# A post-norm layer with linear attention and eight routed experts: row transfers issued by fours, the norms' roots by a power on GpSimd, and merged VectorE instructions

## The chip, the cores and the metric

The kernel runs on one core of one Trainium2 chip. A core has five engines that run their own instruction streams and meet only at semaphores: TensorE (PE, matrix products; its weight loads are listed as PEld), VectorE (DVE), ScalarE (ACT), GpSimd (POOL) and SyncE (SP, which here only issues transfers). The metric is the device time of one execution in microseconds (us); lower is better.

## The reference, cut to what matters

The input is 4 sequences of 512 tokens with 256 features, all in float32.

```python
Q = relu(x @ Wq.T + bq); K = relu(x @ Wk.T + bk); V = x @ Wv.T + bv     # 16 heads of 16
Q, K = Q * decay, K * decay
KV = einsum('bhnd,bhne->bhde', K, V);  Ksum = K.sum(axis=2)
Z = 1 / (einsum('bhnd,bhd->bhn', Q, Ksum) + EPS)
a = (einsum('bhnd,bhde->bhne', Q, KV) * Z) @ Wo.T + bo
x1 = layernorm(x + a)                                      # (v - mean) / sqrt(var + 1e-5)
probs = softmax(x1 @ w_gate); the two largest of 8 experts, their weights made to sum to 1
routed = sum over the two of weight * (silu(g) * u) @ w_down[e],   g, u = x1 @ w_gate_up[e]
shared = (silu(gs) * us) @ w_sh_down,                              gs, us = x1 @ w_sh_gate_up
out = layernorm(x1 + routed + shared)
```

## The kernel before, in words

Float32 products are made of three products of a high and a low part (`split3`, lines 332 to 334), so nearly every operand is first copied into a high part by ScalarE or GpSimd and then subtracted into a low part by VectorE or GpSimd. The order of work on each engine is written out by hand; no scheduler moves anything, and each engine takes its own list in order.

**Attention.** A loop runs over the four sequences b = 0 to 3. On TensorE sequence b has `k_t_v` (L373), the key and value products of sequence b+1, `attend` (L387) for its four tiles of 128 tokens, `proj_q` of b+1, `o_transposed` (L400), `x1_transposed` of b-1 (L426), `proj_o` and the `router` of b-1 (L437). In sequence 3, which has no successor, the first pieces of the shared expert (`shared_gu`) stand between these. VectorE does `kvm_out` (masks the key-value product, L960 and L961, needed by `attend`), `o_out` for each tile (L969, L970, L974), `ot_lo_out` (L985), and `moments`, which adds the residual (L999) and takes mean and variance (L994, L1005). Then comes `x1_norm`, a chain of 12 VectorE instructions on 4 columns that finds 1/sqrt(var + eps) by an integer guess and three Newton steps (`rstd`, L214 to L227). ScalarE's `x1_apply` (L710) applies it. The call of `x1_norm` for sequences 0 and 1 stands in the middle of the next sequence's `o_out`, for sequence 2 ahead of `kvm_out` of sequence 3, and for sequence 3 behind its `moments`.

**Routing and rows.** `top_two` (L1014 to L1030) picks two experts a token, `ranks` on TensorE (L449, L451) counts them, `slots` (L1069 to L1078) turns that into row numbers. GpSimd's `scatter(b)` then writes every token's row of 1032 bytes to two places in HBM: eight indirect transfers of 128 rows (L1318), one behind the other. In between GpSimd splits the feed-forward weights (`split_chunk`, L1301 and L1303, 18 chunks), and makes low parts (`x1_lo`, L1309). SyncE waits for all scatters before it loads the first tile of expert rows (L298).

**Shared expert.** For each sequence four column blocks: `shared_gu` on TensorE, `shared_sg` (L729) on ScalarE, `shared_h` (L1039) on VectorE, `shared_hh` (L736) on ScalarE, `shared_lo` (L1045) on VectorE, then `shared_dn` on TensorE and `shared_out` (L1057) on VectorE, which adds tile by tile into `x1`. Sequences 0 and 1 come before the routed experts, 2 and 3 after them.

**Experts and end.** 40 tiles of 128 rows run through gate, up and down products; results are scattered back (L1345), added up (L1358, L1222), and the second norm is taken: on GpSimd for sequences 0 to 2 by the same Newton steps in 16 instructions each time, on VectorE for sequence 3 (L214 to L227 again), then applied (L859, L1237) and stored (L321).

Of the kernel before, what the change touches and what calls it, by code (L numbers as in the profile page):

```python
# [10 lines left out]
I32 = mybir.dt.int32  # L11
U32 = mybir.dt.uint32
ALU = mybir.AluOpType
# [3 lines left out]
P = 128  # L17
NB, SEQ, D = 4, 512, 256
KD = D // P
# [44 lines left out]
RSQRT_MAGIC = 0x5F3759DF  # L64


def build(nc, xT, x, watt, batt, bq, wffn, wgate, consts, out):
# [5 lines left out]
    with ctx:  # L73
# [36 lines left out]
        warm = sb("warm", [P, 2])  # L110
        stat = sb("stat", [P, TB, 6])
# [98 lines left out]
        def rstd(v, link, h, fused):  # L210


            va, y, t, m = (nw[:, h, n, :] for n in range(4))
            link(v.tensor_scalar(va, mv[:, h, :, 1], EPS_LN, None, ALU.add))  # L214
            link(v.tensor_scalar(y.bitcast(I32), va.bitcast(I32), -0.5, float(RSQRT_MAGIC), ALU.mult, ALU.add))
            for _ in range(3):
                if fused:
                    link(v.scalar_tensor_tensor(t, y, -0.5, y, ALU.mult, ALU.mult))
                    link(v.tensor_tensor(t, t, va, ALU.mult))  # L219
                    link(v.scalar_tensor_tensor(y, t, 1.5, y, ALU.add, ALU.mult))  # L220
                else:
                    link(v.tensor_tensor(t, y, y, ALU.mult))
                    link(v.tensor_tensor(t, t, va, ALU.mult))
                    link(v.tensor_scalar(t, t, -0.5, 1.5, ALU.mult, ALU.add))
                    link(v.tensor_tensor(y, t, y, ALU.mult))
            if fused:
                return v.scalar_tensor_tensor(m, mv[:, h, :, 0], -1.0, y, ALU.mult, ALU.mult)  # L227
            link(v.tensor_tensor(m, mv[:, h, :, 0], y, ALU.mult))
            return v.tensor_scalar(m, m, -1.0, None, ALU.mult)
# [97 lines left out]
        def _(pe):  # L327
# [292 lines left out]
            pe.wait_ge(S["sres_out"], EARLY_B * TB)  # L620
# [278 lines left out]
        def _(dve):  # L899
# [53 lines left out]
            def kvm_out(b):  # L953
# [4 lines left out]
                for m in range(KD):  # L958
                    o = bank[4][:, m * (P + 1):(m + 1) * (P + 1)]
                    v.tensor_tensor(kvm[:, m, 0:P], o[:, 0:P], blk, ALU.mult)  # L960
                    last = v.tensor_scalar(kvm[:, m, P:P + HB], headm, o[:, P:P + 1], None, ALU.mult)  # L961
                last.then_inc(S["kvm_out"], 1)

            def o_out(b, t):

# [454 lines left out]
```

## Time and profile before

| what | us |
|---|---|
| median of 3 runs | 292.87 (292.04 to 293.07) |
| span of the profiled execution, first to last instruction | 284.3 |
| median less span | 8.6 |
| PE busy | 233.3 (82%) |
| DVE busy | 170.2 (60%) |
| POOL busy | 143.5 (50%) |
| ACT busy | 123.3 (43%) |
| mean granted TensorE clock | 0.930 |

Of the profiled execution only the span is shown; a time of its own around it is not. A row of the timeline has start, duration, engine, line, operation, what it writes and reads, the shape and the count, and in brackets how long the engine had stood idle before it and what ended that. "remote" there means that the releasing update could not be tied to an instruction near it. Ends of matmuls are modelled. TensorE, the busiest engine, still stands idle or runs at half its clock in several places, and the table of waits says who ends each pause.

### The profile page before, as it was taken

The page shows a single profiled execution, that of the slowest core. Times are in us where ns is not written, and L with a number is a line of the kernel's source. Part 1 is how long each engine was busy: PE and PEld are TensorE (multiplying, and loading weights), DVE is VectorE, ACT ScalarE, POOL GpSimd, SP SyncE. Part 2 cuts the span into 40 slices and gives each one's busy share as a digit, 9 for nine tenths or more (in the row PEclk, how much of TensorE's full clock was granted, in tenths as well). Part 3 has the DMA queues.
Part 4 walks back from the last instruction along what each step waited for, and adds up shares of the span by engine and source line. Part 5 has one row for each costly group of instructions (what it writes and reads, how often), then busy time and mean ns, then how long its engine had stood idle before and what let it go on. Part 6 is the DMA issues. An engine that isn't in the chain of part 4 may idle for free.

```text
span 284.3 us, 5136 instructions
## 1 busy us (share of the span) xinstructions
PE 233.3 (82%) x1420; PEld 199.2 (70%) x1420; DVE 170.2 (60%) x603; ACT 123.3 (43%) x315; POOL 143.5 (50%) x176
## 2 busy tenths in 40 slices
PE   8799999699794779298783889999999889995370
PEld 3488798598593659285763878888888778894370
DVE  2915467369738857637936256666655524699635
ACT  2252613903630370432024166666765634832730
POOL 0035583797779047258740015665655560748700
PEclk9889999999988699879997899999999999999685
DMA  6913064223421002112352025455554306650242
GB/s 192 379 55 94 0 204 168 75 74 111 129 98 37 2 0 106 42 59 93 120 178 77 0 74 164 139 165 149 162 149 152 109 11 205 241 149 0 71 152 74
DMA packets 21580, 31.72 MB, mean 112 GB/s; under 512 B 3248, under 2 KB 14257, under 8 KB 21556
## 3 DMA queue, kind: packets, MB, share of 16 engines
q1 hardware_dynamic: 17552, 22.46, 26.0%
q0 software_dynamic: 3456, 8.43, 8.6%
q10 hardware_dynamic: 548, 0.53, 0.6%
q8 instruction: 13, 0.21, 0.3%
q14 instruction: 11, 0.09, 0.1%
HBM read 19.70 MB, written 12.76 MB: 114 GB/s over the span
## 4 chain that ended last, share of the span: by engine, by line
PE 54%; DVE 21%; issue 10%; ACT 6%; another core or an unknown queue 6%; DMA 2%; ACTq 0%; DVEq 0%
PE bank L332 16%; PE bank L334 13%; PE bank L333 12%; PE bank L578 3%; PE bank L373 2%; DVE stat L1230 2%; DVE nw L219 2%; DMA k_sb<-in_batt 2%; PE bank L599 2%; ACT xt_hi L736 2%; DVE xt_raw L1039 2%; PE bank L426 1%; DVE x L1222 1%; PE bank L437 1%
## 5 line engine op out<-in xcount | busy, mean ns | idle before, releaser
L1345 POOL DMA_INDIRECT y_pairs<-x_t,dst x40 | 39.4, 985 | 49.1 <-ACT x_t L814 24.9
L332 PE MATMUL bank<-wf_hi,ot_hi 128*128 x120 | 41.1, 342 | 4.1 <-DVE ot_lo L1183 3.0
L1318 POOL DMA_INDIRECT x_slots<-x,slot x32 | 31.7, 991 | 17.6 <-DVE slot L1078 8.9
L332 PE MATMUL bank<-wf_hi,xt_hi 128*128 128x256 f32 x64 | 20.4, 319 | 16.4 <-DVE xt_lo L1045 10.7
L333 PE MATMUL bank<-wf_lo,ot_hi 128*128 x120 | 33.8, 282 | 0.0
L334 PE MATMUL bank<-wf_hi,ot_lo 128*128 x120 | 33.8, 281 | 0.0
L332 PEld LDWEIGHTS bank<-wf_hi,ot_hi 128*128 128x128 f32 x120 | 22.5, 188 | 10.9 <-issue 9.9
L332 PE MATMUL bank<-x1t_hi,wf_hi 128*128 128x512 f32 x64 | 26.7, 418 | 1.2 <-ACT x_t L719 1.2
L332 PEld LDWEIGHTS bank<-wf_hi,xt_hi 128*128 128x128 f32 x64 | 14.2, 223 | 17.6 <-issue 17.6
L333 PE MATMUL bank<-x1t_lo,wf_hi 128*128 128x512 f32 x64 | 25.9, 405 | 0.0
L736 ACT CAST xt_hi<-xt_raw 128x512 fp32r<-128x512 f32 x16 | 9.7, 618 | 37.3 <-remote 11.9
L334 PE MATMUL bank<-x1t_hi,wf_lo 128*128 128x512 f32 x64 | 25.8, 403 | 0.0
L1303 POOL TENSOR_TENSOR wf_lo<-stage,wf_hi 128x512 fp32r<-128x512 f32 x18 | 23.2, 1287 | 1.4
L333 PEld LDWEIGHTS bank<-wf_lo,ot_hi 128*128 128x128 f32 x120 | 22.8, 190 | 0.0
L334 PEld LDWEIGHTS bank<-wf_hi,ot_lo 128*128 128x128 f32 x120 | 22.6, 188 | 0.0
L685 ACT ACTIVATE k_sb<-bank,cst 128x256 f32<-128x256 f32 x16 | 7.6, 475 | 33.7 <-PE bank L348 33.2
L1181 DVE SCALAR_TENSOR_TENSOR dst<-o_sb,te_f 128x1 f32 (+1 forms) x40 | 8.8, 221 | 19.5 <-issue 13.7
L333 PE MATMUL bank<-wf_lo,xt_hi 128*128 128x256 f32 x64 | 19.9, 311 | 0.0
L334 PE MATMUL bank<-wf_hi,xt_lo 128*128 128x256 f32 x64 | 19.8, 310 | 0.0
L804 ACT ACTIVATE q_t<-bank 128x128 f32<-128x128 f32 x40 | 11.1, 278 | 19.9 <-PE bank L334 19.9
L799 ACT CAST ot_hi<-bank 128x256 fp32r<-128x256 f32 x40 | 15.0, 378 | 9.2 <-PE bank L578 8.8
L1293 POOL TENSOR_TENSOR xt_lo<-xt_raw,xt_hi 128x512 fp32r<-128x512 f32 x6 | 7.5, 1276 | 18.4 <-ACT xt_hi L676 18.4
(179 smaller groups left out, 648.8 us busy)
## 6 DMA issues: line engine op xcount, KB each, us to landing
o_sb<-x_slots SPq DMA_DIRECT2D x40, 129.0 KB
stage<-in_wffn SPq DMA_DIRECT2D x18, 256.0 KB, 2.8
x<-in_x SPq DMA_DIRECT2D x4, 512.0 KB, 7.1
out<-x SPq DMA_DIRECT2D x8, 256.0 KB, 2.3
xt_raw<-in_xT SPq DMA_DIRECT2D x3, 512.0 KB, 6.4
x_slots<-fill SPq DMA_DIRECT2D x9, 129.0 KB, 4.5
x<-in_watt SPq DMA_DIRECT2D x4, 256.0 KB, 5.9
k_sb<-y_pairs SPq DMA_DIRECT2D x2, 512.0 KB, 3.7
```

Of the source, the lines that this page charges most:

```text
L332: mm(o, w_hi, m_hi, start=start, stop=False, **more)
L333: mm(o, w_hi, m_lo, start=False, stop=False, **more)
L334: return mm(o, w_lo, m_hi, start=False, stop=stop, **more)
L578: last = nc.tensor.transpose(o[:, k * P:(k + 1) * P], xg[:, u, k * P:(k + 1) * P], ident)
L685: activation(k_sb[:, t, :], o[:, 0:D], ACT.Relu, scale=cst[:, C_DEC + t:C_DEC + t + 1])
L736: copy(hh_hi[:, c, :], hf[:, i % 2, :]).then_inc(S["shh_out"], 1)
L799: copy(xe_hi[:, u % 2, :, :], bank[(4, 7)[u % 2]][:, 0:KD * P].rearrange("p (k n) -> p k n", k=KD)).then_inc(S["xe_hi_out"], 1)
L804: activation(eg[:, u % 2, :], bank[u % 2][:, 0:IM], ACT.Silu).then_inc(S["eg_out"], 1)
L1181: v.scalar_tensor_tensor(dst[:, bass.ds(j, 1)], xg[:, u, D + 1:DT], te_f[:, bass.ds(j + (RING - 1), 1)], xg[:, u, D:D + 1], ALU.not_equal, ...
L1303: g.tensor_tensor(wf_lo[:, c], stage[:, i % 2, :], wf_hi[:, c].bitcast(F32), ALU.subtract).then_inc(S["wf_split"], 1)
L1318: pool.indirect_dma_start(out=x_scat, out_offset=bass.IndirectOffsetOnAxis(ap=slot[:, j, t:t + 1], axis=0), in_=x1[:, t, :], in_offset=Non ...
L1345: pool.indirect_dma_start(out=y_scat, out_offset=bass.IndirectOffsetOnAxis(ap=dst[:, j:j + 1], axis=0), in_=ey[:, u, :], in_offset=None, b ...
```

## The change

Four edits. (1) The chain in `rstd` becomes four GpSimd instructions, one of them a power with exponent -0.5 from a new constant tile; all norms, those of the attention and the last one included, are now GpSimd's, each at a fixed place in its list. (2) `scatter(b)` is cut into two parts of four transfers. Those of sequence 0 have other work between them. From sequence 1 on, GpSimd waits until a part has landed (`landed`) before it issues the next. (3) `kvm_out` makes two instructions in place of four, `o_out` one product for each tile in place of two. (4) `shared_out` adds two tiles at once, and the semaphore `sres_out` counts pairs.

```diff
+        power = sb("power", [P, NB, TB])
-        def rstd(v, link, h, fused):
-            va, y, t, m = (nw[:, h, n, :] for n in range(4))
-            link(v.tensor_scalar(va, mv[:, h, :, 1], EPS_LN, None, ALU.add))
-            link(v.tensor_scalar(y.bitcast(I32), va.bitcast(I32), -0.5, float(RSQRT_MAGIC), ALU.mult, ALU.add))
-            for _ in range(3):
-                if fused:
-                    link(v.scalar_tensor_tensor(t, y, -0.5, y, ALU.mult, ALU.mult))
-                    link(v.tensor_tensor(t, t, va, ALU.mult))
-                    link(v.scalar_tensor_tensor(y, t, 1.5, y, ALU.add, ALU.mult))
...
+        def rstd(g, link, h):
+            va, y, m = nw[:, h, 0, :], nw[:, h, 1, :], nw[:, h, 3, :]
+            link(g.tensor_scalar(va, mv[:, h, :, 1], EPS_LN, None, ALU.add),
+                 g.tensor_scalar(m, mv[:, h, :, 0], -1.0, None, ALU.mult))
+            link(g.tensor_tensor(y, va, power[:, h, :], ALU.pow))
+            return g.tensor_tensor(m, m, y, ALU.mult)
...
-                        pe.wait_ge(S["sres_out"], TB * (b - 1) + 2 * (t // 2) + 2)
+                        pe.wait_ge(S["sres_out"], 2 * (b - 1) + t // 2 + 1)
...
+                o = bank[4][:, 0:KD * (P + 1)].rearrange("p (m n) -> p m n", m=KD)
+                v.tensor_tensor(kvm[:, :, 0:P], o[:, :, 0:P], blk.unsqueeze(1).broadcast_to([P, KD, P]), ALU.mult)
+                v.tensor_tensor(kvm[:, :, P:P + HB], o[:, :, P:P + 1].broadcast_to([P, KD, HB]),
+                                headm.unsqueeze(1).broadcast_to([P, KD, HB]), ALU.mult).then_inc(S["kvm_out"], 1)
...
+                v.tensor_tensor(o_sb[:, t, 0:D].rearrange("p (k h e) -> p k h e", k=KD, h=HB),
+                                o[:, :, 0:P].rearrange("p k (h e) -> p k h e", h=HB),
+                                zt.unsqueeze(3).broadcast_to([P, KD, HB, DH]), ALU.mult).then_inc(S["o_out"], 1)
...
-            x1_norm(b - 1)
             kvm_out(b)
             top_two(b - 2)
...
+            def landed(b, part):
+                pool.wait_ge(S[f"scattered{b}"], 16 * TOPK * (TB // 2) * (part + 1))
...
                     if b == 2 and n == 4:
-                        scatter(0)
+                        scatter(0, 0)
                         x1_lo(b - 1)
+                        x1_norm(2)
                     split_chunk(done)
                     done += 1
+                    if b == 2 and n == 4:
+                        scatter(0, 1)
...
+                    if n == 5 and b == 0:
+                        x1_norm(0)
                     if n == 3 and b == 1:
                         x1_lo(b - 1)
+                        x1_norm(1)
+            scatter(1, 0)
             x1_lo(NB - 2)
-            scatter(1)
-            scatter(2)
+            x1_norm(3)
+            landed(1, 0)
+            scatter(1, 1)
+            landed(1, 1)
+            scatter(2, 0)
             x1_lo(NB - 1)
-            scatter(3)
+            landed(2, 0)
+            scatter(2, 1)
+            landed(2, 1)
+            scatter(3, 0)
+            landed(3, 0)
+            scatter(3, 1)
...
+            pool.wait_ge(S["bn_out"], 4 * TB)
+            rstd(g, link, slice(3, 4)).then_inc(S["ln_last_out"], 1)
```

How this moves instructions, in two places. First VectorE at the mask of sequence 3 (kvm). Before, from the last Newton step of sequence 2's norm (nw, the last four of its twelve instructions) to the router's copy (logit):

```order
L218 SCALAR_TENSOR_TENSOR nw<-nw 128x4 [waits dve_chain]
L219 TENSOR_TENSOR nw<-nw 128x4 [waits dve_chain]
L220 SCALAR_TENSOR_TENSOR nw<-nw 128x4 [waits dve_chain]
L227 SCALAR_TENSOR_TENSOR nw<-mv,nw 128x4 [waits dve_chain]
L960 TENSOR_TENSOR kvm<-bank,cst 128x128 [waits num_mm,kvp_mm]
L961 TENSOR_SCALAR kvm<-cst,bank 128x8
L960 TENSOR_TENSOR kvm<-bank,cst 128x128
L961 TENSOR_SCALAR kvm<-cst,bank 128x8
L1014 COPY logit<-bank 128x32 [waits lg_mm]
```

And after, from the moments (BN_AGGR) of sequence 2 on:

```order
L988 BN_AGGR mv<-stat 128x2 x3
L946 TENSOR_TENSOR kvm<-bank,cst 128x2x128 [waits num_mm,kvp_mm]
L947 TENSOR_TENSOR kvm<-bank,cst 128x2x8
L993 COPY logit<-bank 128x32 [waits lg_mm]
L997 MAX top_v<-logit 128x8 [waits lg_out]
```

The twelve norm instructions are gone from in front of the mask, and the mask is two instructions long. Second GpSimd from its 17th weight chunk to the experts, where x_slots is the scatters' target, x1t_lo a low part and nw a norm. Before:

```order
L1303 TENSOR_TENSOR wf_lo<-stage,wf_hi 128x512 [waits wf_split]
L1309 TENSOR_TENSOR x1t_lo<-x_t,x1t_hi 128x512 [waits x1hi_out]
L1309 TENSOR_TENSOR x1t_lo<-x_t,x1t_hi 128x512
L1318 DMA x_slots<-x,slot 17536x258 [waits x1_out,tags_out,slots_out]
L1318 DMA x_slots<-x,slot 17536x258 x7
L1318 DMA x_slots<-x,slot 17536x258 [waits x1_out,tags_out,slots_out]
L1318 DMA x_slots<-x,slot 17536x258 x7
```

And after, for the same work and up to the first part of sequence 2:

```order
L1281 TENSOR_TENSOR wf_lo<-stage,wf_hi 128x512 [waits wf_split]
L1300 DMA x_slots<-x,slot 17536x258 [waits x1_out,tags_out,slots_out]
L1300 DMA x_slots<-x,slot 17536x258 x3
L1287 TENSOR_TENSOR x1t_lo<-x_t,x1t_hi 128x512 [waits x1hi_out]
L1287 TENSOR_TENSOR x1t_lo<-x_t,x1t_hi 128x512
L213 TENSOR_SCALAR nw<-mv 128x4 [waits mom_out]
L214 TENSOR_SCALAR nw<-mv 128x4
L215 TENSOR_TENSOR nw<-nw,power 128x4 [waits pool_chain]
L216 TENSOR_TENSOR nw<-nw 128x4 [waits pool_chain]
L1300 DMA x_slots<-x,slot 17536x258 [waits scattered1]
L1300 DMA x_slots<-x,slot 17536x258 x3
L1300 DMA x_slots<-x,slot 17536x258 [waits tags_out,x1_out,slots_out,scattered1]
```

The norm of sequence 3 now stands between the two halves of the scatter of sequence 1, so the second half can't start before sequence 3's moments are there, and each later half waits for the landing of the one before.

## Rows read from the trace of the kernel before

**Rows 1.** Waits of TensorE, whole span: total us, times, longest us.

```profile
PE bank L332 <- DVE xt_lo L1045: 10.7, 2, 7.6
PE bank L332 <- DVE x L1057: 5.7, 1, 5.7
PE bank L387 <- DVE kvm L961: 5.5, 1, 5.5
PE bank L426 <- ACT x L710: 5.1, 1, 5.1
```

**Rows 2.** Timeline of ScalarE: x1_apply of sequences 0, 1 and 2.

```profile
49.46 2.08 ACT L710 ACTIVATE x<-x,nw 128x256 f32<-128x256 f32 x4 [1.28 <-DVE nw L227]
73.81 2.08 ACT L710 ACTIVATE x<-x,nw 128x256 f32<-128x256 f32 x4 [2.51 <-DVE nw L227]
93.36 2.07 ACT L710 ACTIVATE x<-x,nw 128x256 f32<-128x256 f32 x4 [11.97 <-DVE nw L227]
```

**Rows 3.** Timeline of VectorE: norm of sequence 2, then the mask.

```profile
87.39 1.18 DVE L214 TENSOR_SCALAR nw<-mv 128x4 f32<-128x4 f32 x1
...
93.25 0.29 DVE L960 TENSOR_TENSOR kvm<-bank,cst 128x128 f32<-128x128 f32 x1
```

**Rows 4.** Timeline of TensorE around attend of sequence 3.

```profile
88.18 0.40 PE L334 MATMUL bank<-x1t_hi,wf_lo 128*128 128x512 f32 x1
94.07 2.18 PE L387 MATMUL bank<-kvm,q_t 128*128 128x136 f32 x8 [5.50 <-DVE kvm L961]
```

**Rows 5.** Timeline of GpSimd: the x1_lo in the norm's time, scatter 1's fifth and last.

```profile
85.99 2.54 POOL L1309 TENSOR_TENSOR x1t_lo<-x_t,x1t_hi 128x512 fp32r<-128x512 f32 x2
...
110.70 0.96 POOL L1318 DMA_INDIRECT x_slots<-x,slot  x1 [0.30 <-issue]
...
114.51 0.96 POOL L1318 DMA_INDIRECT x_slots<-x,slot  x1 [0.31 <-issue]
```

**Rows 6.** Timeline of TensorE, 109.8 to 142.6: router, shared blocks, first products of shared_dn.

```profile
109.82 1.84 PE L437 MATMUL bank<-wg_sb,x_t 128*128 128x8 f32 x16
...
114.15 0.39 PE L334 MATMUL bank<-x1t_hi,wf_lo 128*128 128x512 f32 x1
...
142.58 0.28 PE L334 MATMUL bank<-wf_hi,xt_lo 128*128 128x256 f32 x1
```

**Rows 7.** Timeline of VectorE: a residual add, the router's copy, the slot cast.

```profile
110.02 0.42 DVE L999 TENSOR_TENSOR x<-bank,x 128x256 f32<-128x256 f32 x1
...
116.92 0.19 DVE L1014 COPY logit<-bank 128x32 f32<-128x32 f32 x1 [2.38 <-remote]
...
132.33 3.12 DVE L1078 CAST slot<-slot_f 128x8 uint32<-128x8 f32 x1
```

**Rows 8.** Timeline of ScalarE: shared blocks that wait for TensorE.

```profile
117.05 0.60 ACT L729 ACTIVATE xt_raw<-bank 128x512 f32<-128x512 f32 x1 [1.85 <-remote]
...
147.41 1.14 ACT L736 CAST xt_hi<-xt_raw 128x512 fp32r<-128x512 f32 x2 [11.94 <-remote]
```

**Rows 9.** Windows: length, busy of PE, PEld, DVE, ACT, POOL, PEclk, DMA share, GB/s.

```profile
116.00:117.00 1.00, 0.00 (x0) 0.00 (x0) 0.08 (x1) 0.00 (x0) 0.00 (x0) 1.00 0.37 132
```

**Rows 10.** The same columns, in stretches of 2 us.

```profile
120.00:122.00 2.00, 2.00 (x14) 1.94 (x13) 0.94 (x4) 0.34 (x1) 0.00 (x0) 0.50 0.00 0
...
134.00:136.00 2.00, 0.00 (x0) 0.00 (x0) 2.00 (x3) 1.08 (x2) 1.68 (x3) 1.00 0.00 0
```

**Rows 11.** Timeline of SyncE: first loads of expert tiles.

```profile
150.29 14.37 SPq L298 DMA_DIRECT2D o_sb<-x_slots  x5
```

**Rows 12.** Timeline of VectorE at the end: the last norm's first and last instruction.

```profile
277.85 0.17 DVE L214 TENSOR_SCALAR nw<-mv 128x4 f32<-128x4 f32 x1
...
280.03 0.16 DVE L227 SCALAR_TENSOR_TENSOR nw<-mv,nw 128x4 f32<-128x4 f32 x1
```

**Rows 13.** Timeline of GpSimd: two norm instructions on 4 columns.

```profile
269.19 0.20 POOL L223 TENSOR_TENSOR nw<-nw 128x4 f32<-128x4 f32 x1
269.47 0.19 POOL L224 TENSOR_SCALAR nw<-nw 128x4 f32<-128x4 f32 x1
```

More of the change, by code:

```diff
@@ L972, in o_out @@
                     dve.wait_ge(S["ot_mm"], b)
-                for m in range(KD):
-                    last = v.tensor_tensor(
-                        o_sb[:, t, m * P:(m + 1) * P].rearrange("p (h e) -> p h e", h=HB),
-                        o[:, m, 0:P].rearrange("p (h e) -> p h e", h=HB),
-                        zt[:, m, :].unsqueeze(2).broadcast_to([P, HB, DH]), ALU.mult)
-                last.then_inc(S["o_out"], 1)
+                v.tensor_tensor(o_sb[:, t, 0:D].rearrange("p (k h e) -> p k h e", k=KD, h=HB),
+                                o[:, :, 0:P].rearrange("p k (h e) -> p k h e", h=HB),
+                                zt.unsqueeze(3).broadcast_to([P, KD, HB, DH]), ALU.mult).then_inc(S["o_out"], 1)
             def ot_lo_out(b):
@@ L1127, in _ @@
                     o_out(b, t)
-                    if b >= 1 and t == 1:
-                        x1_norm(b - 1)
                     if b >= 2 and t == 2:
@@ L1276, in _, with link, x1_norm @@
             g.memset(fill[:, 0:D], 0.0).then_inc(S["pool_chain"], 1)
+            g.memset(power[:, :, :], -0.5).then_inc(S["pool_chain"], 1)
             pool.wait_ge(S["cst_in"], 16)
             g.tensor_copy(fill[:, D:DT], cst[:, C_FILL:C_FILL + TAG]).then_inc(S["pool_chain"], 1)
-            pool.wait_ge(S["pool_chain"], 2)
+            pool.wait_ge(S["pool_chain"], 3)
             pool.sem_inc(S["fill_made"], 1)
-            chain = [2]
-            def link(ins):
-                chain[0] += 1
-                ins.then_inc(S["pool_chain"], 1)
+            chain = [3]
+            def link(*instructions):
+                for ins in instructions:
+                    chain[0] += 1
+                    ins.then_inc(S["pool_chain"], 1)
                 pool.wait_ge(S["pool_chain"], chain[0])
+            def x1_norm(b):
+                pool.wait_ge(S["mom_out"], TB * (b + 1))
+                rstd(g, link, slice(b, b + 1)).then_inc(S["nw_last_out" if b == NB - 1 else "nw_out"], 1)
             def split_x_lo(b):
@@ L1310, in x1_lo, with scatter @@
                                     ALU.subtract).then_inc(S["x1lo_out"], 1)
-            def scatter(b):
-                pool.wait_ge(S["slots_out"], b + 1)
-                pool.wait_ge(S["tags_out"], 2 * (b + 1))
-                pool.wait_ge(S["x1_out"], TB * (b + 1))
-                for t in range(b * TB, (b + 1) * TB):
+            def scatter(b, part):
+                if part == 0:
+                    pool.wait_ge(S["slots_out"], b + 1)
+                    pool.wait_ge(S["tags_out"], 2 * (b + 1))
+                    pool.wait_ge(S["x1_out"], TB * (b + 1))
+                half = TB // 2
+                first = b * TB + part * half
+                for t in range(first, first + half):
                     for j in range(TOPK):
```

45 lines of the change are left out of this document (11 added, 34 removed).

## The prediction

> **What bounds the kernel now.** I read the waits of TensorE first, then the timelines of the engines that end them, in order of time. The profile's page has TensorE busy for 233.3 of the span's 284.3 us, so a gain must come from its pauses and from stretches at the lower clock. Its long pauses are few: 5.5 us for the mask, 5.1 us for the applied norm, 5.7 us for the shared addition, and twice for the shared expert's low part, once 7.6 us in the tail and once the other 3.1 us [rows 1]. Each has a cause behind the engine named.
>
> The mask (5.5 us) stands behind sequence 2's norm on VectorE, which runs from 87.39 to 93.25, 5.9 us for twelve tiny instructions [rows 3]; one such chain undisturbed takes 2.34 us (277.85 to 280.19) [rows 12]. Its first instruction took 1.18 us in place of 0.17 [rows 3, 12], while GpSimd ran 512-column subtractions [rows 5]. The chain is held by GpSimd's work, so its price on VectorE is 2.4 to 5.9 us a time.
>
> The next pauses share a stranger cause: TensorE's completions arrive late. The router's products were recorded from 109.82 to 111.66 and shared_gu's last one to 114.54 [rows 6]. VectorE was free, but copied the logits only at 116.92 [rows 7], and ScalarE's SiLU began at 117.05 [rows 8], 2.5 us after its product. A residual add that waited for TensorE at 110.02 came on time [rows 7]. What changed between is the fifth of eight row transfers, issued at 110.70; the eighth was issued at 114.51 [rows 5], and its 132 KB moved in 116 to 117 [rows 9]. So lateness begins with the fifth transfer in a row and ends when they have all landed. It repeats in the last scatter: shared_dn's last product ended at 142.86 [rows 6], ScalarE's cast that waited for it ran at 147.41 [rows 8].
>
> **The change part by part.** The sum is made in the profiled span of 284.3 us. I take the 8.6 us between it and the median of 292.87 as constant, so what leaves the span leaves the median.
>
> *Norm 0.* In sequence 1 ScalarE stood idle for 1.28 us for the norm [rows 2], and TensorE waited behind ScalarE. On GpSimd the norm stands behind the sixth weight chunk, in an idle stretch, and is ready earlier. Gain 1.3 (0 to 1.3).
>
> *Norm 1.* The same, with 2.51 us of ScalarE's idle time [rows 2]. Also VectorE no longer holds back the slots and the last o_out, for which TensorE waited. It works without pause before and behind, so not all comes back. I take 2.2 (0 to 3).
>
> *Norm 2 and the mask.* TensorE's last product ahead of attend began at 88.18, and attend itself at 94.07 [rows 4], 5.9 us later. The mask's input came from TensorE earlier, so attend starts at about 88.2. It took 2.18 us [rows 4] at the lower clock; without the pause the clock should not have fallen, which halves that. Gain 5.9 + 1.1, and 0.1 for the merged mask: 7.1 (4 to 7.5). What is late next? The norm itself: GpSimd has four transfers (each 1.3 us), x1_lo of 2.54 us [rows 5], then the norm. By this count its result is there at 88.5 in place of 93.3, and ScalarE's x1_apply (2.07 us [rows 2]) ends at 90.6, ahead of the transposition that needs it. The lower end is that GpSimd is 3 us later.
>
> *Groups of four, at 114.5.* If no more than four transfers are in a row, completions are on time. SiLU goes from 117.05 to 114.6: 2.4 us (0 to 2.5). The pause before the transposition shrinks from 5.1 us [rows 1] to 2.7. In the pause of 3.1 us later the granted clock stayed 1.00 (2.4 GHz), behind the one of 5.1 us it was 0.50 (1.2 GHz) [rows 10]. TensorE works all through that stretch [rows 10], by my count for 4.8 us, of which full clock gives back at most half; a part is bound by weight loads. I take 2.1 (0 to 2.4).
>
> *At 133.7.* shared_dn waited 3.1 us for the low part. VectorE had the ranks late, and then its slot cast took 3.12 us [rows 7], held by an x1_lo that followed the scatter directly. In the new order the ranks are on time, and x1_lo falls ahead of TensorE's need. Gain 3.0 (0 to 3.1).
>
> *At 142.9 to 154.1.* ScalarE's cast moves from 147.41 to 142.9. Counted on through the next two blocks (product, SiLU, product with the gate, cast, low part) the shared addition is 2.2 us earlier, 0 if lateness stays. The pause of 5.7 us [rows 1] becomes 3.5. Whether the clock then stays up lies between the two pauses above; the slow products there cost about as much as those above, I take 0.9 (0 to 2.2).
>
> *The last norm.* VectorE: 2.34 us [rows 12]. GpSimd: an instruction on 4 columns takes 0.20 us and the next begins 0.28 us after it [rows 13], so four take 1.1 us. The power is not in the trace. Its lower bound is 0.20 like the others, its upper bound a whole 512-column instruction, 1.3 us [rows 5]. It has only 4 columns, so I take 0.4, near the small rows: 1.3 us and a gain of 1.0 (0 to 1.2). The norms of sequences 0 to 2 in the tail are hidden behind shared blocks.
>
> *Merged products.* o_out lies beside TensorE's products nearly everywhere; if that cover goes it is 0.07 us a tile. Three shared_out calls stand on the path. With both, 0.1 (0 to 0.3).
>
> *The new waits.* The fourth transfer lands 2.5 us after its issue, as the eighth at 114.51 did by 117.0 [rows 5, 9]. A group then takes 3 x 1.27 + 2.5 = 6.3 us against 5.1 unhindered. Queued behind are x1_lo of sequence 3 and the later groups; SyncE waits for the last before the first expert tile. From norm 3 (at about 102 in the new time) there are five groups, 31.5 us, and 2.5 us of x1_lo: tiles could be loaded from 136, and be there at 138. TensorE ends shared_dn(1) at about 140. Before, the loads began at 150.29 [rows 11] and TensorE's need was at 162. So the cover shrinks from 10 us to 2, and the cost is 0 (0 to 3).
>
> The Trainium skill (DMA: Bandwidth & Descriptors, section Anatomy of one DMA) gives about 2.0 us as the fixed cost of a transfer from GpSimd, most of it the receipt of the write, which speaks against waiting for landings. The trace has 2.5 us with the data, and by the page's figure the five groups would be 2 us shorter, which changes no term. Its GPSIMD Engine Reference (4.1 Engine selection) advises VectorE for elementwise work, GpSimd being about twice as slow with two inputs. By that rule the last norm would take 1.6 us, and the gain 0.7 in place of 1.0; on 4 columns the trace has 0.20 against 0.17 us [rows 12, 13], so here the count of instructions decides.
>
> Sum: 1.3 + 2.2 + 7.1 + 2.4 + 2.1 + 3.0 + 2.2 + 0.9 + 1.0 + 0.1 = 22.3 us. 284.3 becomes 262.0, and 292.87 becomes 270.6.
>
> **The rivals.**
>
> *Completions stay late.* Then the terms 2.4, 2.1, 3.0, 2.2 and 0.9 (10.6 us) are void, and the time is 281.2. For it speaks that each transfer lands before the third behind it is issued, so four are hardly ever in flight together, and a limit on what is in flight would not explain the fifth; the halves of a scatter also come close together. Against it: in the rows the releases fall at the landing, which a pause for landing should bring about each time. 18%.
>
> *GpSimd's list is late.* Norm 2 waits behind four transfers and x1_lo, norm 3 behind part of scatter 1, and what follows waits for landings. If each norm comes 2 to 3 us after I think, some 5 us are lost: 275.5. For it: GpSimd is busy for nearly all of 70 to 92. 15%.
>
> *The pauses still bring the clock down,* or TensorE takes up new small waits after each: the clock terms of 1.1, 2.1 and 0.9 are gone: 274.7. 12%.
>
> *Code for the power is loaded first.* If this costs some us once, at norm 0, it eats ScalarE's slack there (x1_apply could begin at 48.2 [rows 2], some 4 us behind the norm), and for a load of 6 us the time is 272. The Trainium skill (GPSIMD Engine Reference, 2.1 Instruction dispatch) states such a first load of about 6 us for a freshly loaded kernel; no row here shows one. 3%.
>
> *Slower: the power is slow.* Norms 2, 3 and the last stand on the path. With C us for each power the last loses C - 1.2, the others what is over their slack of some 3 and 2 us. Three times C less 6 reaches the 22.3 us gained at C of 9.5, and from there the kernel is slower; at 12 us it is 300. A GpSimd instruction on 128 times as many elements takes 1.3 us [rows 5], which speaks against it. 4%.
>
> **How the numbers follow.** The forecast has 48%: 270.6, by itself 267 to 274. The upper bounds of all terms together are 25.7 us, or 267.2, hence the low end, half a microsecond under; the late completions at 281.2 are taken in with half a microsecond over. The range is 266.5 to 282. Changes within 0.5% of 292.87 (1.5 us) are what a measurement of this kernel can't tell from none. All cases but the slow power are faster by more; I leave 3% for gains that other waits take over whole and 5% for slower: 92%, 3%, 5%.
>
> **What would show it.** Right: attend of sequence 3 starts within 0.5 us of the shared products ahead of it; no VectorE or ScalarE wait for TensorE is ended by "remote" during the scatters; four norm instructions on GpSimd within 1.5 us; PEclk without the dip behind sequence 3's norm; the first expert tiles loaded before shared_dn(1) ends. Wrong: logits copied long after the router's last product, a power of over 1 us, GpSimd issuing row transfers while TensorE waits for a tile, or a pause of over 1 us before x1_transposed of sequence 2.

## The result, and the profile after

The changed kernel took 274.06 us (median of 4 runs, 273.05 to 274.88) beside 292.59 us before (292.04 to 293.07): a ratio of 0.941, 95% interval 0.937 to 0.946. Its profiled execution took 273.63 us with a span of 271.8 us. The forecast was 270.6 us in a range of 266.5 to 282. The time lies in the range, but not for all the reasons given: the trace of after is 12.5 us shorter than that of before (284.3), not 22.3, and the rest of the 18.5 us between the medians is in neither trace. Here and below, a ratio compares only the fast runs, those within 1.5% of each kernel's fastest, so it can differ from the ratio of the medians.

First the waits of TensorE in the changed kernel, whole span (total us, times, longest us), against [rows 1]:

```profile
PE bank L319 <- DVE xt_lo L1024: 8.3, 2, 7.4
PE bank L319 <- DVE ot_lo L1157: 4.8, 7, 0.9
PE bank L319 <- DVE x L1035: 3.5, 1, 3.5
PE bank L565 <- DMA o_sb<-x_slots: 3.2, 2, 2.7
PE bank L413 <- ACT x L697: 2.6, 1, 2.6
```

L319 is a product of a high or low part, L565 the transposition of an expert tile. The wait for the mask is gone, the one for the applied norm fell from 5.1 to 2.6 us, that for the shared addition from 5.7 to 3.5. New is the wait for the first expert tiles (o_sb from x_slots, 3.2 us), and the waits for the experts' low part (ot_lo) are seven.

The middle of the kernel, from the timelines of ScalarE, TensorE and VectorE (start us, us, engine, line, operation):

```profile
46.30 2.09 ACT L697 ACTIVATE x<-x,nw 128x256 f32<-128x256 f32 x4
68.54 2.08 ACT L697 ACTIVATE x<-x,nw 128x256 f32<-128x256 f32 x4
...
83.43 1.09 ACT L697 ACTIVATE x<-x,nw 128x256 f32<-128x256 f32 x2 [7.64 <-POOL nw L216]
...
82.98 0.28 PE L374 MATMUL bank<-kvm,q_t 128*128 128x136 f32 x1
...
106.36 0.33 PE L413 MATMUL bank<-cst,x 128*128 128x128 f32 x1 [2.65 <-ACT x L697]
...
110.78 0.19 DVE L993 COPY logit<-bank 128x32 f32<-128x32 f32 x1 [1.35 <-PE bank L424]
```

ScalarE no longer stands idle for the norms of sequences 0 and 1 [rows 2]. Attend of sequence 3 starts at 82.98, in the place of 94.07 [rows 4], with no wait, and the transposition of sequence 3's x1 at 106.36 in the place of 119.66, where before had its wait of 5.1 us [rows 1]: 13.3 us saved, 13.0 forecast up to there. The logits of sequence 2 are copied when TensorE is done, and no wait here is ended by "remote" any more [rows 7].

The end, from the timelines of VectorE, GpSimd and SyncE, against [rows 12, 13]:

```profile
263.21 0.38 DVE L1207 BATCH_NORM_AGGREGATE mv<-stat 128x2 f32<-128x6 f32 x4
263.68 0.23 POOL L213 TENSOR_SCALAR nw<-mv 128x4 f32<-128x4 f32 x1 [13.37 <-DVE mv L1207]
263.99 0.23 POOL L214 TENSOR_SCALAR nw<-mv 128x4 f32<-128x4 f32 x1
264.30 1.04 POOL L215 TENSOR_TENSOR nw<-nw,power 128x4 f32<-128x4 f32 x1
265.41 0.20 POOL L216 TENSOR_TENSOR nw<-nw 128x4 f32<-128x4 f32 x1
265.65 1.06 DVE L1211 TENSOR_SCALAR x<-x,nw 128x256 f32<-128x256 f32 x3 [2.06 <-POOL nw L216]
266.41 0.89 SPq L308 DMA_DIRECT2D out<-x  x2
```

And windows behind it (us; busy us of PE, PEld, DVE, ACT, POOL; granted clock, DMA share, GB/s):

```profile
266.00:269.00 3.00, 0.00 (x0) 0.00 (x0) 0.70 (x3) 0.25 (x1) 0.00 (x0) 0.50 0.52 175
269.00:272.00 3.00, 0.00 (x0) 0.00 (x0) 0.00 (x0) 0.00 (x0) 0.00 (x0) 0.50 0.00 0
```

The power on 4 columns took 1.04 us, five times its neighbours, and the four instructions took 1.93 us. Of the signs that the prediction had named, one for wrong came (a power of over 1 us) and two for right did not: a norm within 1.5 us, and tile loads ahead of the end of shared_dn(1). They began at 140.61, and TensorE had stood still since 140.0. And the last 2.8 us of the span are empty: no engine works and no byte moves. In the kernel before, the span ended 4.1 us behind the last apply, here 6.2 us.

Where the 12.5 us of the two spans come from, by places that both traces have:

| place | before | after | saved so far | forecast so far |
|---|---|---|---|---|
| attend of sequence 3 | 94.07 | 82.98 | 11.1 | 9.4 |
| transposition of sequence 3's x1 | 119.66 | 106.36 | 13.3 | 13.0 |
| first expert tile's cast | 162.6 | 143.5 | 19.1 | 21.2 |
| last expert output | 231.9 | 217.1 | 14.8 | 21.2 |
| last apply | 280.23 | 265.65 | 14.6 | 22.3 |
| end of the span | 284.3 | 271.8 | 12.5 | 22.3 |

### The profile page after: what moved, and what is told of

Its sections match the earlier page's. It is cut to its first block, busy times and chain, and to the rows that moved or that the text cites. A ratio compares the mean times of both kernels' runs of the same rounds, so it can differ in the third digit from the quotient of the medians.

```text
span 271.8 us, 5043 instructions
## 1 busy us (share of the span) xinstructions
PE 227.2 (84%) x1420; PEld 194.4 (72%) x1420; DVE 150.2 (55%) x511; ACT 123.1 (45%) x315; POOL 148.8 (55%) x173
## 4 chain that ended last, share of the span: by engine, by line
PE 55%; DVE 17%; issue 9%; DMA 6%; ACT 6%; POOL 4%; SPq 1%; DVEq 0%; ACTq 0%; POOLq 0%
PE bank L319 15%; PE bank L321 13%; PE bank L320 12%; DMA x_slots<-x,slot 4%; PE bank L565 4%; POOL x_slots L1300 3%; PE bank L360 3%; PE bank L424 2%; DVE stat L1204 2%; DVE x L1196 2%; DMA k_sb<-in_batt 2%; DVE ot_lo L968 1%; PE bank L586 1%; PE bank L374 1%; DVE xt_raw L1018 1%
## 5 line engine op out<-in xcount | busy, mean ns | idle before, releaser
L319 PE MATMUL bank<-wf_hi,ot_hi 128*128 x120 | 42.0, 350 | 5.7 <-DVE ot_lo L1157 4.8
L321 PE MATMUL bank<-wf_hi,ot_lo 128*128 x120 | 34.5, 287 | 0.0
L319 PEld LDWEIGHTS bank<-wf_hi,ot_hi 128*128 128x128 f32 x120 | 23.4, 195 | 12.3 <-issue 11.3
L319 PE MATMUL bank<-wf_hi,xt_hi 128*128 128x256 f32 x64 | 19.7, 307 | 11.8 <-DVE xt_lo L1024 8.3
L319 PE MATMUL bank<-x1t_hi,wf_hi 128*128 128x512 f32 x64 | 25.9, 405 | 1.2 <-ACT x_t L706 1.2
L320 PE MATMUL bank<-x1t_lo,wf_hi 128*128 128x512 f32 x64 | 25.2, 394 | 0.0
L320 PEld LDWEIGHTS bank<-wf_lo,ot_hi 128*128 128x128 f32 x120 | 23.5, 196 | 0.0
L321 PEld LDWEIGHTS bank<-wf_hi,ot_lo 128*128 128x128 f32 x120 | 23.3, 194 | 0.0
L319 PEld LDWEIGHTS bank<-wf_hi,xt_hi 128*128 128x128 f32 x64 | 13.5, 212 | 13.0 <-issue 13.0
L565 PE MATMUL bank<-cst,o_sb 128*128 128x128 f32 x80 | 16.8, 293 | 3.4 <-DMA o_sb<-x_slots 3.2
```

Source lines behind the costliest of these rows:

```text
L319: mm(o, w_hi, m_hi, start=start, stop=False, **more)
L320: mm(o, w_hi, m_lo, start=False, stop=False, **more)
L321: return mm(o, w_lo, m_hi, start=False, stop=stop, **more)
L565: last = nc.tensor.transpose(o[:, k * P:(k + 1) * P], xg[:, u, k * P:(k + 1) * P], ident)
```

## The experiments

The kernel before ran beside every set. Its own median was the first surprise:

| set | kernel before, us | variants, us |
|---|---|---|
| the result | 292.6 (4 runs, 292.0 to 293.1) | changed 274.1 |
| A | 277.1 (23 runs, 271.1 to 285.9) | groups 277.5, norms 271.7, merges 277.5, no waits 269.5 |
| B | 290.0 (14 runs, 283.7 to 292.7) | changed 272.8, three waits 278.1, Newton 282.5 |
| C | 277.4 (17 runs, 273.8 to 282.9) | changed 269.6, groups 276.4, norms 270.6, no waits 268.8 |
| D | 278.4 (11 runs, 273.0 to 281.9) | no waits 271.4 |

Sets A and B ran on one and the same chip, C on a second, D on a third; for the result's set the chip is not on record. In each run that lists both, the time is 1.8 to 1.9 us above the span. Below, A, C and D are called the early sets (before at 277 to 278), the result's set and B the late ones (before at 290 to 293). The names stand for completions of TensorE that are on time or late. In the nine traces of A, C and D no wait of VectorE or ScalarE is ended by "remote". Before's trace has five such waits; of the four in the late sets, the changed kernel in B and the one with three waits have one each, the changed kernel's first and the one with Newton's steps none. No set has a trace of before taken in it, so that late completions are what makes before slow in a late set is inferred.

**Groups of four alone (set A).** The kernel before with the change's order of GpSimd's list and its landing waits, and nothing else:

```diff
-            x1_lo(NB - 2); scatter(1); scatter(2); x1_lo(NB - 1); scatter(3)
+            scatter(1, 0); x1_lo(NB - 2); landed(1, 0); scatter(1, 1)
+            landed(1, 1); scatter(2, 0); x1_lo(NB - 1); landed(2, 0); scatter(2, 1)
+            landed(2, 1); scatter(3, 0); landed(3, 0); scatter(3, 1)
```

> The kernel before with one part of the change: the row transfers in groups of four, with the waits for the landing; all norms stay on VectorE, no merged products. My theory (late completions of TensorE last from the fifth transfer in a row to the landing, so groups of four cure them): the logits of sequence 2 are copied within 0.5 us of the router's product, no wait of VectorE or ScalarE for TensorE is ended by 'remote' during the transfers, the mask's pause of some 5.5 us stays. Time: 292.6 less the 10.6 us of the group terms, plus some 3 us for the wait for the first expert tile: 283 to 286. Rival (the norms' move did the work, the groups only cost): 292 to 296, slower, with completions still 2 us late.

Measured: 277.51 us, ratio 0.997 (0.989 to 1.006): nothing gained. Both theories had taken before at 292.6, which it was not here, and the mechanism is judged by the traces below. One thing expected of the trace failed: the mask's pause does not stay. In this trace, and in that of the same edit in set C, TensorE does not wait for kvm. Norm 2's first instruction on VectorE, the mask and attend in set C:

```profile
84.27 0.17 DVE L214 TENSOR_SCALAR nw<-mv 128x4 f32<-128x4 f32 x1
...
86.55 0.29 DVE L960 TENSOR_TENSOR kvm<-bank,cst 128x128 f32<-128x128 f32 x1
...
87.51 1.09 PE L387 MATMUL bank<-kvm,q_t 128*128 128x136 f32 x8
```

From the first of the twelve instructions to the mask it is 2.3 us in place of 5.9 [rows 3]: with the scatter cut in two, GpSimd's x1_lo is over (at 82.3) before they begin. In the trace of the merges alone, where an x1_lo runs beside them (87.13 to 89.65), their second instruction takes 3.16 us and TensorE waits 5.0 us for the mask. So this edit holds more than its name says, and either of two edits, the groups or the norms' move, removes that pause.

**Norms alone (set A).** The changed kernel with nothing merged and

```diff
-            scatter(1, 0); x1_lo(NB - 2); x1_norm(3); landed(1, 0); scatter(1, 1); ...
+            x1_lo(NB - 2); x1_norm(3); scatter(1); scatter(2); x1_lo(NB - 1); scatter(3)
```

> The changed kernel with the transfers again in eights and without landing waits, and without the merged products: only the norms are moved to GpSimd. My theory: the mask's pause is gone (attend of sequence 3 directly behind the shared products) but completions come 2 us late or more from the fifth transfer on; 292.6 less 1.3, 2.2, 7.1 and some 0.4 for the last norm is 281.6, range 280 to 284. Rival (with the norms away, VectorE's list is no longer late and the transfers hurt nobody): 274 to 277, as fast as the changed kernel.

Measured: 271.67 us, ratio 0.994 (0.986 to 1.001), 0.6% by the ratio, which is not clear of none, and 5.4 us in the medians; before scatters by 15 us here. The trace has no wait for the mask, as expected, and no late completion, where 2 us or more were expected.

**Merges alone (set A).** The kernel before with the mask, o_out and shared_out merged:

```diff
-                for t in range(TB):
+                for h in range(TB // 2):
...
-                    v.tensor_tensor(r, shared_sum(t), r, ALU.add
+                    v.tensor_tensor(r, bank[5 + h][:, :].rearrange("p (i d) -> p i d", i=2), r, ALU.add
```

> The kernel before with the merged products and additions alone (mask, attention products, shared additions on two tiles). My theory: they lie beside TensorE's work, 0 to 0.5 us faster, 292.1 to 292.6. Rival (the longer addition over two tiles makes those wait that need only the first, and the later signal costs): 0.5 to 1.5 us slower.

Measured: 277.50 us beside 277.09: no difference that can be seen. No ratio is on record for it. Its trace says more than its time, because it still sends rows in eights and has the norms on VectorE. The fifth and the eighth transfer of sequence 1, the router's product, the copy of its result, and SiLU's and the norm's turn:

```profile
111.87 0.96 POOL L1313 DMA_INDIRECT x_slots<-x,slot  x1 [0.30 <-issue]
...
115.65 0.96 POOL L1313 DMA_INDIRECT x_slots<-x,slot  x1 [0.30 <-issue]
...
110.97 1.84 PE L437 MATMUL bank<-wg_sb,x_t 128*128 128x8 f32 x16
...
115.62 0.18 DVE L1010 COPY logit<-bank 128x32 f32<-128x32 f32 x1
...
116.26 0.59 ACT L729 ACTIVATE xt_raw<-bank 128x512 f32<-128x512 f32 x1
118.86 1.09 PE L426 MATMUL bank<-cst,x 128*128 128x128 f32 x8 [3.17 <-ACT x L710]
```

The copy had no idle time ahead of it, and both it and the SiLU ran before the eighth transfer, issued at 115.65, can have landed (some 2.5 us behind its issue, by [rows 5, 9]). In the trace of before the same two stood until that landing [rows 7, 8]. TensorE's pause is 3.2 us in place of 5.1. The SiLU's product ended at 115.7 (its last one began at 115.30), so that completion took at most 0.6 us. So eight transfers in a row do not by themselves hold completions back.

**No landing waits (set A).**

```diff
-            landed(1, 0)
...
-            landed(3, 0)
```

> The changed kernel without its five waits for the landing; the groups keep their places, so the transfers of sequence 1's second half and sequence 2's first stand eight in a row, and sequence 2's second half and sequence 3 twelve. My theory: completions are late again, most in sequence 3's part (shared_dn's last product, ScalarE's cast 3 to 5 us behind it), so 3 to 6 us lost; the wait of 3 us for the first expert tile goes; together 273 to 278. Rival (it is the split and the other places of the groups that help, not the waits): no completion late by over 1 us, the tile there in time, 270 to 271.5.

Measured: 269.52 us, ratio 0.986 (0.977 to 0.995). The time is just under the rival's 270 to 271.5. In this early set the rival had it right: no wait of VectorE or ScalarE is ended by "remote", and TensorE does not wait for the first tile.

**The changed kernel again, no edit (set B).**

> The changed kernel as it is, once more, beside the kernel before, since before took 277 us in the runs of the experiments so far and 292.6 beside the first runs of the changed one. Theory (a machine state makes TensorE's completions late during the transfers, the landing waits keep the changed kernel clear of it): where before is at 292 it stays at 274 again; where before is at 277, without late completions, the changed kernel stays at 272 to 274, so the ratio is about 0.985. Rival (the one machine is slower in all things): the ratio of 0.94 holds, and where before is at 277 the changed kernel is at 261.

Measured: 272.81 us beside 289.98, ratio 0.957 (0.950 to 0.964). Before stood 13 us higher than in set A, on the same chip, and the changed kernel where it had been beside the result, so one side of the theory is confirmed. Its trace shows a late completion all the same, during transfers in fours. Last product of shared_dn, last transfer of the group, the cast that waits (all of set B's changed kernel):

```profile
131.40 0.28 PE L321 MATMUL bank<-wf_hi,xt_lo 128*128 128x256 f32 x1
...
132.36 0.96 POOL L1300 DMA_INDIRECT x_slots<-x,slot  x1 [0.30 <-issue]
...
134.29 1.14 ACT L723 CAST xt_hi<-xt_raw 128x512 fp32r<-128x512 f32 x2 [7.73 <-remote]
```

The cast came 2.6 us after the product's end. So even four in a row don't prevent lateness. It ended 1.9 us behind the group's last issue, while GpSimd stood for the landing.

**Three of five waits (set B).**

```diff
-            landed(2, 1)
             scatter(3, 0)
-            landed(3, 0)
```

> The changed kernel with three of its five landing waits (ahead of the second half of sequence 1, ahead of the first and of the second half of sequence 2); sequence 3 is sent at once. Theory (the last waits cost the 2.7 us that TensorE waits for the first expert tile, and the clock behind that): 2.7 us and 1 to 2 us of clock are gained where completions are not late, 269 to 271; where they are late, 0 to 2 us are lost. Rival (the tile's wait is hidden or replaced by another): no difference to the changed kernel.

Measured: 278.10 us, ratio to before 0.976 (0.969 to 0.983), 5.3 us behind the changed kernel where 0 to 2 were expected. The twelve transfers from 120.46 to 135.21 now run without a pause. The same three places:

```profile
130.78 0.28 PE L321 MATMUL bank<-wf_hi,xt_lo 128*128 128x256 f32 x1
...
135.21 0.96 POOL L1300 DMA_INDIRECT x_slots<-x,slot  x1 [0.30 <-issue]
...
137.83 1.14 ACT L723 CAST xt_hi<-xt_raw 128x512 fp32r<-128x512 f32 x2 [11.88 <-remote]
```

Released 6.8 us after the product's end, and 2.6 us after the last issue, as before's 117.0 is 2.5 us behind its eighth [rows 5, 7]. Without two of the waits this completion came 4.2 us later, which is most of the 5.3. The times show what these two waits are worth in a late set; that it is this completion rests on one trace of each kernel. The side that spoke of completions on time, 269 to 271, was not met.

**Newton's steps on GpSimd (set B).** The changed kernel with 16 small instructions a norm:

```diff
-            link(g.tensor_tensor(y, va, power[:, h, :], ALU.pow))
+            link(v.tensor_scalar(y.bitcast(I32), va.bitcast(I32), -0.5, float(RSQRT_MAGIC), ALU.mult, ALU.add))
+            for _ in range(3):
+                link(v.tensor_tensor(t, y, y, ALU.mult))
...
```

> The changed kernel with the norms on GpSimd in the same places, but the roots by the three Newton steps of before: 16 small instructions in a chain in place of four. Each takes about 0.28 us on GpSimd, so a norm takes some 4.5 us instead of 1.9. Theory: the last norm is on the path, 2.5 us lost; norm 2 has ScalarE waiting but TensorE little, 0 to 2 us; the others hidden: 3 to 5 us slower than the changed kernel. Rival (the place alone counts, the power is worth nothing): within 1 us of it.

Measured: 282.52 us, ratio 0.989 (0.983 to 0.994), 9.7 us behind the changed kernel, twice what was expected. Norm 2 on GpSimd and who waits for it, the pause of the next sequence, and the last norm's end:

```profile
84.48 0.27 POOL L214 TENSOR_SCALAR nw<-mv 128x4 f32<-128x4 f32 x1
...
88.83 0.23 POOL L222 TENSOR_SCALAR nw<-nw 128x4 f32<-128x4 f32 x1
...
91.21 1.97 PE L419 MATMUL bank<-cst,x 128*128 128x128 f32 x8 [4.39 <-ACT x L703]
112.92 1.97 PE L419 MATMUL bank<-cst,x 128*128 128x128 f32 x8 [5.39 <-ACT x L703]
...
272.21 0.23 POOL L222 TENSOR_SCALAR nw<-nw 128x4 f32<-128x4 f32 x1
```

A norm takes 4.6 us. TensorE waits 4.4 and 5.4 us for x1_apply, where the changed kernel has one pause of 2.6: 7.2 us more. The last norm, from its aggregate to the apply, stands 4.60 us in place of 2.06, 2.5 us more. Together that is the 9.7 us. So more than half of what the whole change gains over before in this set hangs on the short chain.

**The changed kernel, a third time, no edit (set C).**

> The changed kernel as it is, beside the next three on the same chip. The kernel before has so far been at 277 us beside some runs and at 290 us beside others. Theory (in some stretches of time on the chip TensorE's completions come late while row transfers run, in others not, and the landing waits keep the changed kernel clear of it): 271 to 275 wherever before stands. Rival (it moves with before): near 262 where before is at 277.

Measured: 269.62 us beside 277.44, ratio 0.976 (0.970 to 0.983): neither 271 to 275 nor 262, but 3 us below set B where before was 13 us lower, and on another chip. The same completion as above was on time here (its product began at 129.62):

```profile
130.00 1.14 ACT L723 CAST xt_hi<-xt_raw 128x512 fp32r<-128x512 f32 x2 [5.21 <-PE bank L321]
```

**Groups alone, as in set A (set C).**

> Groups of four with landing waits alone, norms on VectorE, no merged products, as once before. Where the kernel before is at 290: theory (the landing waits are what cures the late completions): 276 to 281, most of the gain, as it was at 277.5 beside a before of 277. Rival (the norms' move is what counts in that case too): 286 or more. Where before is at 277: within 1 us of it again.

Measured: 276.42 us, ratio 1.002 (0.996 to 1.007): in an early set the groups give nothing. In this trace TensorE waits 3.2 us for the first tiles, as in the changed kernel's first one; in the trace of the same edit in set A it does not:

```profile
PE bank L578 <- DMA o_sb<-x_slots: 3.2, 2, 2.8
```

**Norms alone, as in set A (set C).**

> Norms moved to GpSimd alone, transfers in eights without landing waits, no merged products, as once before. Where the kernel before is at 290: theory (late completions stay): 281 to 286, some 5 to 8 us faster than before. Rival (with VectorE's list relieved the late completions hurt nobody): 272 to 275. Where before is at 277: 271 to 273 again.

Measured: 270.57 us, ratio 0.980 (0.973 to 0.987): by the medians 6.9 of the 7.8 us that the whole change gains in this set, by the ratios 2.0 of 2.4%. Neither the norms nor the groups alone were run in a late set, so how the 18.5 us of the result divide between them is not shown.

**No landing waits, as in set A (sets C and D).**

> The changed kernel without its five landing waits, as once before. Where the kernel before is at 290: theory (nothing keeps it clear of late completions): 279 to 285, slower than the changed kernel by 6 us or more; the variant with three waits was at 278.1 beside a changed kernel at 272.8. Rival (the split and the places suffice): 268 to 271. Where before is at 277: 268 to 271 again, some 3 us faster than the changed kernel, since the tile is not waited for.

Measured: 268.82 us, ratio 0.972 (0.964 to 0.979), beside 0.976 (0.970 to 0.983) for the changed kernel: no difference that can be told.

> The changed kernel without its five landing waits, a third time, for the case that the kernel before stands at 290 us beside it, which it did beside two of the four sets of runs so far. Theory (late completions are a condition of the machine, and the landing waits keep the changed kernel, 272.8 us there, mostly clear of it; with three waits it took 278.1): where before is at 290, 279 to 285. Rival (the norms' move and the other places of the groups do it): 270 to 274 where before is at 290. Where before is at 277: 268 to 270, as twice before.

Measured: 271.35 us beside 278.35, ratio 0.985 (0.975 to 0.996), where 268 to 270 were expected. The set was an early one again, so what this kernel does where before is at 290 us stays untried.

## Why the prediction was right, and where it was not

**Norms and mask (10.6 us).** Right in mechanism and about in size: 11.1 us saved at attend against 9.4. Norms alone are worth 2.0% in set C, and in set A 0.6%, which is not clear of none. That GpSimd's work held the chain is borne out by the groups alone: 2.3 us for the chain where no x1_lo ran beside it, and no pause for the mask. So that pause was not the norms' place alone. The rival of a late GpSimd list did not come: sequence 2's x1_apply began at 83.43, and the only pause of TensorE for an applied norm is the one at 106.36. Nor did the one of code loaded first: the first power began 0.1 us behind the instruction ahead of it (at 42.10) and took 1.04 us like the later ones on 4 columns.

**The clock (1.1, 2.1 and 0.9).** The term of 2.1 came in the result's trace and not as a rule. TensorE pauses 2.65 us for sequence 3's applied norm in all three traces of the changed kernel. Behind it the granted clock stayed at 1.00 in the first and was 0.50, that is 1.2 GHz, in those of sets B and C (below, the first and set C's; PEclk is the third number from the end):

```profile
108.00:110.00 2.00, 2.00 (x16) 1.82 (x14) 1.33 (x5) 1.97 (x5) 0.38 (x1) 1.00 0.23 74
```

```profile
108.00:110.00 2.00, 2.00 (x5) 1.61 (x6) 1.51 (x6) 1.97 (x4) 0.19 (x1) 0.50 0.19 66
```

So the step from one pause of 3.1 us with the clock up to a clock that stays up behind one of 2.7 held in one trace of three, which was luck. The terms of 1.1 and 0.9 came in the first trace: the clock was 1.00 in attend and behind the shared addition, until the wait for the tile.

**Groups of four (10.6 us, clock terms of 2.1 and 0.9 included).** The step "if no more than four transfers are in a row, completions are on time" is wrong as a rule. Three things were missed. Before's own trace has two late completions that don't fit the rule, both on VectorE:

```profile
85.85 0.42 DVE L999 TENSOR_TENSOR x<-bank,x 128x256 f32<-128x256 f32 x1 [2.08 <-remote]
...
131.52 0.17 DVE L1069 TENSOR_TENSOR base<-bank,base 128x8 f32<-128x8 f32 x1 [1.83 <-remote]
```

The first waited for a product that ended at 83.4, and ran 0.8 us behind the eighth issue of its scatter (85.02), too soon for a landing 2.5 us behind it; the add before it came on time with six issued. The second waited for one that ended at 129.5, and ran before its scatter's eighth was issued (131.90). So lateness neither begins with the fifth transfer nor always lasts until the last has landed. Then lateness comes and goes between traces: with eight in a row it was absent in the trace of the merges alone. And it can strike within a group of four too (2.6 us in set B). What the waits do is to bound it: 2.6 us with the wait, 6.8 without, in one trace each. That the completion is late and not the product is seen in before: TensorE had begun the twelve products behind the router's by 114.15 [rows 6], and the logits were copied at 116.92 [rows 7]. What holds it back no run shows. The rival that completions stay late (18%) was half right for that reason. The saving between the transposition and the first expert tile was 5.8 us (19.1 less 13.3) against 8.2 forecast.

**The new waits (0, up to 3).** The upper end was right: 3.2 us for the tiles in the first trace (0.6 in set B's, none in set C's). Groups took 6.7 to 8.3 us from first issue to first issue (the 7.5 holds an x1_lo), not 6.3, as these rows show (GpSimd, first transfer of each group in the changed kernel):

```profile
102.90 1.09 POOL L1300 DMA_INDIRECT x_slots<-x,slot  x1 [0.16 <-issue]
...
109.62 0.95 POOL L1300 DMA_INDIRECT x_slots<-x,slot  x1 [1.84 <-DMA x_slots<-x,slot]
```

The first tile was asked for at 140.61, not 136. (In the prediction's aside on a fixed cost of 2.0 us, half a microsecond less for each of five groups is 2.5 us, not 2; nothing hangs on it.)

**The experts, which no term spoke of.** From the first tile's cast to the last output the traces have (duration ns min/median/max, first and last start us), before, then changed, then changed in set C:

```profile
L799 ACT CAST ot_hi<-bank x40: 372/378/415, 162.6 to 227.0; 128x256 fp32r<-128x256 f32 x40
L814 ACT COPY x_t<-bank x40: 372/372/402, 168.1 to 231.9; 128x256 f32<-128x256 f32 x40
```

```profile
L786 ACT CAST ot_hi<-bank x40: 372/378/432, 143.5 to 212.1; 128x256 fp32r<-128x256 f32 x40
L801 ACT COPY x_t<-bank x40: 372/372/418, 150.4 to 217.1; 128x256 f32<-128x256 f32 x40
```

```profile
L786 ACT CAST ot_hi<-bank x40: 372/378/382, 146.6 to 209.9; 128x256 fp32r<-128x256 f32 x40
L801 ACT COPY x_t<-bank x40: 372/373/377, 152.0 to 214.7; 128x256 f32<-128x256 f32 x40
```

That is 69.3, 73.6 and 68.1 us. The 4.3 us lost in the first trace are the clock and small waits. TensorE stood for the tiles, and the clock that had been low ahead of the experts in before was low inside them (before, then after):

```profile
154.00:158.00 4.00, 3.87 (x18) 3.90 (x19) 1.15 (x5) 0.12 (x1) 0.00 (x0) 0.50 0.16 49
162.00:170.00 8.00, 6.38 (x49) 5.42 (x47) 4.94 (x19) 5.04 (x15) 0.77 (x1) 1.00 0.23 66
```

```profile
143.00:151.00 8.00, 7.16 (x37) 6.28 (x36) 3.49 (x13) 4.59 (x12) 0.00 (x0) 0.60 0.37 94
```

At 0.60 for 8 us some 3 us of full clock are missing; the waits for ot_lo grew from 3.0 to 4.8 us. In set C the same kernel had no wait for a tile and lost nothing here. The loads are no earlier there, 140.14 against 140.61; it is TensorE that comes later. With the clock up behind sequence 3's norm, and without a pause of 2.5 us for hot_m that set C's trace has, it was 5.0 us ahead at shared_dn's pause for the shared addition (over at 133.99 against 138.96), wanted the first tile at 140.0, before it was asked for, and then lost the lead to the tile and the low clock behind it. In set C it began on the tile at 146.1 with no wait, and the whole kernel was 3.0 us shorter (span 268.8). Time gained ahead of the experts is worth no more than the row transfers let through.

**The last norm (1.0).** Wrong by 2.7 us. The power was taken at 0.4 and measured at 1.04, so from the aggregate's end to the apply it is 2.06 us against 2.41: 0.35 gained, within the bounds. But the end of the span moved from 4.1 to 6.2 us behind the apply, a cost without a term. It goes with GpSimd: from the start of GpSimd's last instruction to the end of the span it is 6.4 us in the changed kernel (265.41 to 271.8) and 6.5 with Newton's steps (272.21 to 278.7). Where VectorE makes the last norm, the span ends 4.1 us behind the last apply (groups alone in set C, span 271.6 us):

```profile
267.52 1.05 DVE L1237 TENSOR_SCALAR x<-x,nw 128x256 f32<-128x256 f32 x3
```

So the last norm's move lost 1.7 us. Back on VectorE, with the rest as changed, should be 1.7 us faster; that version was not run.

**Merged products (0.1).** Nothing measurable, as forecast.

**The step from span to median.** "I take the 8.6 us between it and the median as constant" was the largest single error. Every run here has 1.8 to 1.9 us there. By that the profiled execution of before took about 286.1 us (an estimate from these runs), and the 292.6 beside the changed kernel hold 6.5 us that its trace does not contain. The three numbers add up: 12.5 us between the spans and 6.5 us between executions of before are 19.0, less the 0.4 us by which the traced execution of after is below its median, against 18.5 between the medians. This is bookkeeping: what the 6.5 us consist of no trace shows. From 286.1 the sum would have given 263.8 for an execution that took 273.6, so the sum was 10 us too large; the 6.5 us that the change also took away stood in no term. The two errors partly cancel, and that the forecast lies 3.5 us from the measured time is in part luck.

What stays open: what brings about one condition or the other. Sets A and B were on one chip, with before at 277 and at 290, so it is not the chip alone.

## What to carry to other kernels

Compare the profiled execution's own time with the median before any sum, and run the kernel before beside every variant: here its median moved by 13 us between sets, more than any single edit was worth. What is gained ahead of a stage is worth only as much as that stage's inputs are early: here TensorE came 5 us sooner and stood for a tile. A wait for a landing can be an insurance: it gave nothing where before stood at 277 us, and where before stood at 290 two such waits fewer cost 5.3 us. What is moved to the engine that finishes first may make it the one that ends the program; look at the empty time at the end of the span.

## What the runs showed of the hardware that was not expected

- GpSimd's power costs by the column: 1.04 us on 4 columns, and on 8 twice that:

```profile
245.40 2.07 POOL L215 TENSOR_TENSOR nw<-nw,power 128x8 f32<-128x8 f32 x1
247.56 0.20 POOL L216 TENSOR_TENSOR nw<-nw 128x8 f32<-128x8 f32 x1
```

- Where GpSimd makes the last norm, the span ends 6.4 to 6.5 us after the start of its last instruction, 6.1 to 6.2 us behind the last apply, in all ten traces; where VectorE makes it, 4.0 to 4.1 us behind the last apply, in all four.
- TensorE's completions can reach other engines up to 6.8 us late while GpSimd's row transfers run, in six places of three traces. In four of them they were released 1.9 to 2.6 us after the last issue of a run of transfers, in one 0.8 us after it and in one 0.4 us before it. In another set on the same chip they were on time with seven transfers in a row issued and the eighth to come.
- GpSimd's 512-column subtractions slow tiny VectorE instructions that run beside them: one on 4 columns took 3.16 us in the merges alone, and from the chain's start to the mask it was 7.9 us there, 5.9 in before and 2.3 with none beside it.
- The same pause of TensorE, 2.65 us, left the granted clock at 1.00 in one trace of a kernel and brought it to 0.50 in two others.
